# Attention followed by an expert layer: VectorE turns the summed head outputs in 32x32 blocks, reading the PSUM bank, where TensorE transposed ScalarE's copies of it

## What is computed

```python
y = einsum('bhqk,bhkd->bhqd', softmax(causal(q k^T / 4)), v)
y = y + einsum('bhqk,bhkd->bhqd', softmax(qc kc^T / 4), vc)
x = x + (y.reshape(B, T, C) @ Wp + bp)
x = x + expert_layer(layernorm(x))
```

## Time and profile before

| | |
|---|---|
| median of 3 runs | 1554.93 us |
| the profiled execution | 1567.87 us, its span 1565.1 us |
| PE busy | 1466.7 us (94%) |
| DVE busy | 1124.9 us (72%) |
| ACT busy | 907.4 us (58%) |
| POOL busy | 548.4 us (35%) |

### The profile page before, as it was taken

One profiled execution on the slowest core, in us unless ns is written; L12 is line 12 of the kernel. 1 busy time (PEld: TensorE's weight loads), 2 busy tenths in 40 slices (PEclk: granted clock), 3 DMA queues, 4 the chain that ended last, 5 costly groups with the idle time before them and its releaser, 6 DMA issues. The chain is left out here.

```text
span 1565.1 us, 26271 instructions
## 1 busy us (share of the span) xinstructions
PE 1466.7 (94%) x8868; PEld 717.5 (46%) x8868; DVE 1124.9 (72%) x3134; ACT 907.4 (58%) x1754; POOL 548.4 (35%) x1013
## 2 busy tenths in 40 slices
PE   8899999999999999999999999999998857999997
PEld 4443444444444444444453445344443323676674
DVE  7878887877888788778876887787785067455451
ACT  2177777677777777676777777767776500212211
POOL 4132333352344324332434333333213121443452
PEclk9599999999999999999999999999999877999999
DMA  6766483829374846575466738481900120444442
GB/s 189 121 142 84 89 111 103 118 66 147 101 106 85 144 103 103 98 157 82 91 116 125 100 81 127 106 117 63 138 4 3 42 86 14 117 99 123 119 99 50
DMA packets 82390, 155.25 MB, mean 99 GB/s; under 512 B 13008, under 2 KB 46416, under 8 KB 82256
## 3 DMA queue, kind: packets, MB, share of 16 engines
q1 hardware_dynamic: 74752, 142.43, 47.9%
q0 software_dynamic: 6144, 8.52, 3.2%
q10 hardware_dynamic: 1360, 2.62, 0.4%
HBM read 96.52 MB, written 53.08 MB: 96 GB/s over the span
## 5 line engine op out<-in xcount | busy, mean ns | idle before, releaser
L828 ACT ACTIVATE probs<-bank_ps 128x512 f32<-128x512 f32 (+1 forms) x1408 | 725.2, 579 | 236.7 <-PE bank_ps L610 229.9
L928 DVE TENSOR_REDUCE chunk_max<-bank_ps 128x1 f32<-128x512 f32 x1024 | 652.5, 684 | 125.2 <-PE bank_ps L649 122.4
L610 PE MATMUL bank_ps<-q_stack,k_stack 64*128 64x512 f32 (+3 forms) x1536 | 506.4, 422 | 41.2 <-ACT probs L828 37.3
L649 PE MATMUL bank_ps<-k_stack,q_stack 62*128 62x512 f32 (+3 forms) x1536 | 529.0, 432 | 7.0 <-DVE chunk_max L928 5.1
L649 PEld LDWEIGHTS bank_ps<-k_stack,q_stack 62*128 62x128 f32 x1536 | 248.8, 189 | 361.6 <-DVE chunk_max L928 211.5
L931 DVE CUSTOM_DVE_ANT_0 masked<-bank_ps,causal 128x128 bf16<-128x128 f32 (+3 forms) x512 | 233.4, 485 | 80.6 <-PE bank_ps L649 79.0
L610 PEld LDWEIGHTS bank_ps<-q_stack,k_stack 64*128 64x128 f32 x1536 | 235.1, 187 | 107.2 <-ACT probs L828 99.7
L1101 POOL TENSOR_TENSOR pool_idle<-pool_idle 128x1 f32<-128x1 f32 x292 | 57.0, 195 | 636.2 <-ACT probs L828 291.4
L628 PE MATMUL out_ps<-probs,v_cross 128*32 128x512 f32 x2048 | 277.1, 613 | 0.0
L1437 ACT ACTIVATE h<-h_ps,b1T 128x512 f32<-128x512 f32 x64 | 44.0, 687 | 227.3 <-PE h_ps L1369 227.3
L1369 PE MATMUL h_ps<-ff_yT,w1T 128*128 128x512 f32 x256 | 114.5, 601 | 0.6 <-DVE ff_yT L1450 0.6
(11 more groups left out here) (173 smaller groups left out, 1372.2 us busy)
## 6 DMA issues: line engine op xcount, KB each, us to landing
parts_dram<-parts SPq DMA_DIRECT2D x70, 512.0 KB, 2.7
k_stack<-parts_dram SPq DMA_DIRECT2D x180, 192.0 KB, 11.6
q_stack<-parts_dram SPq DMA_DIRECT2D x180, 128.0 KB, 10.6
w1T<-in_L_ffn_fc1s SPq DMA_DIRECT2D x8, 1024.0 KB, 5.7
w2T<-in_L_ffn_fc2s SPq DMA_DIRECT2D x8, 1024.0 KB, 7.4
z_rows<-z_sb SPq DMA_DIRECT2D x8, 528.0 KB, 13.9
x_sb<-in_x SPq DMA_DIRECT2D x8, 512.0 KB, 4.7
ctxT<-in_ctx SPq DMA_DIRECT2D x8, 512.0 KB, 11.6
```

The source lines that it names most:

```text
L610: mm = pe.matmul(bank_of(turn)[:, of.at:of.end], k_stack[base:base + SIDE, g, pair, of.keys:of.keys + P], q_stack[base:base + SIDE, g, pai ...
L649: return pe.matmul(bank[:, 0:n], q_stack[base:base + MAX_ROWS, g, pair, qc:qc + P], k_stack[base:base + MAX_ROWS, g, pair, k0:k0 + n], sta ...
L828: nc.scalar.activation(probs[:, buffer(u, i, p), side, columns], bank_of(("score", g, i, p, side))[:, columns], ACT.Exp, scale=SCALE)\
L928: nc.vector.tensor_reduce(dst, bank[:, 0:n], AX.X, ALU.max).then_inc(max_done, 1)
```

## The change

The turn of the sums moves from TensorE to VectorE. VectorE's transpose works in blocks of 32x32, in place among the partitions: each head's 32 partitions (16 channels, the denominator, 15 unused) become 32 columns, so the denominators lie along the free dimension as before. A query stands then on another partition than it would after a whole transpose; since a second turn puts it back, only the layouts of y_sb, y_add and rden change. To make the four heads' blocks of a unit fall at the right channels, a unit now holds heads h, h+2, ... of a half (head_in_half), and the loads from parts_dram pick those rows, in the same sizes.

- turn_heads: VectorE transposes out_ps (PSUM) into u_sb, behind maximum ahead_of_pieces of step 2 (causal part of the unit before) and of step 10 (context part). The value products of those steps now wait for turned, VectorE's semaphore. copy_out falls away.
- divide: VectorE's reciprocal and product, now from u_sb, at the places of OUTPUT_PLAN; GpSimd's addition follows at divide_self.
- turn_back: twice a batch VectorE turns y_sb into yT, and ScalarE adds the bias in place in SBUF (add_value_bias), where yT0 and yT1 were.
- The pieces out_cross, out_self, yT0, yT1 are gone, and PLAN is rearranged. Of the 44 steps of a batch, 28 had a piece besides "shift" before, and 19 have one now.
- Behind the loop VectorE also does the last addition; TensorE runs 8 matmuls of ones meanwhile (BEFORE_LAST).

```diff
-    (0, 2): (("vc0", 1),), (0, 3): (("out_cross", 0), ("out_self", 0)), (0, 4): (("v", 1),),
...
-    (3, 0): (("kc1", 1),), (3, 2): (("out_cross", 0),), (3, 3): (("k", 1), ("vc0", 0)), (3, 5): (("qc", 1),),
-    (3, 6): (("out_self", 0), ("zT1", 0)), (3, 7): (("shift", 0),), (3, 8): (("gate", 0), ("vc1", 0)),
+    (0, 2): (("v", 1),), (0, 3): (("vc0", 1),), (0, 5): (("y0T0", 0), ("y0T1", 0)), (0, 6): (("vc1", 1),),
+    (0, 7): (("shift", 0),), (0, 8): (("k", 0),), (0, 9): (("qc", 0),), (1, 1): (("kc1", 0),), (1, 2): (("q", 0),),
+    (1, 4): (("kc0", 0),), (1, 7): (("shift", 0),), (1, 10): (("proj0", 0),), (2, 1): (("proj1", 0),),
+    (2, 4): (("q", 1),), (2, 5): (("v", 0), ("vc0", 0)), (2, 7): (("shift", 0),), (2, 9): (("zT0", 0),),
+    (2, 10): (("kc1", 1), ("zT1", 0)), (3, 2): (("qc", 1),), (3, 3): (("k", 1),), (3, 4): (("kc0", 1), ("vc1", 0)),
+    (3, 6): (("gate", 0),), (3, 7): (("shift", 0),),
+}
+OUTPUT_PLAN = {
+    (0, 3): ("divide_cross",), (0, 5): ("divide_self",), (0, 8): ("turn_back",), (1, 2): ("divide_cross",),
+    (1, 4): ("divide_self",), (2, 3): ("divide_cross",), (2, 4): ("divide_self",), (2, 5): ("turn_back",),
+    (3, 2): ("divide_cross",), (3, 4): ("divide_self",),
 }
...
                 if i in (0, CROSS_IT) and (u > 0 or i > 0):
-                    pe.wait_ge(u_ready, 2 * u + (i > 0))
+                    pe.wait_ge(turned, 2 * u + (i > 0))
...
-            def copy_out(b, g, s):
-
-                u = UNITS * b + g
-                act.wait_ge(pv_done, ITS * u + (ITS if s else CROSS_IT))
...
-                nc.scalar.copy(u_sb[:, s, :], out_ps[:]).then_inc(u_ready, 1)
+            def add_value_bias(b, c):
+
+                act.wait_ge(turned_back, KT * b + c + 1)
+                nc.scalar.activation(yT[:, c, :], yT[:, c, :], ACT.Identity, bias=bias_v[:, 2, c:c + 1])\
+                    .then_inc(y_biased, 1)
...
+            def turn_heads(unit, s):
+
+                dve.wait_ge(pv_done, ITS * unit + (ITS if s else CROSS_IT))
+                nc.vector.transpose(u_sb[:, s], out_ps[:]).then_inc(turned, 1)
+
+            def divide(unit, s):
+
+                sums = u_sb[:, s].rearrange("p (n c) -> p n c", c=BLOCK)
+                dve.wait_ge(turned, 2 * unit + s + 1)
+                nc.vector.reciprocal(rden[:, s], sums[:, :, D]).then_inc(rden_done, 1)
+                if s:
+                    dve.wait_ge(y_done, unit)
+                dve.wait_ge(rden_done, 2 * unit + s + 1)
+                nc.vector.tensor_tensor(y_add[:] if s else heads_of(unit), sums[:, :, 0:D],
+                                        rden[:, s].unsqueeze(2).broadcast_to([P, T // BLOCK, D]),
+                                        ALU.mult).then_inc(y_part, 1)
+
+            def turn_back(b, c):
+
+                dve.wait_ge(y_done, UNITS * b + UNITS_HALF * (c + 1))
+                nc.vector.transpose(yT[:, c], y_sb[:, c].rearrange("p n c -> p (n c)")).then_inc(turned_back, 1)
...
                             if n == ahead_of_pieces(i):
+                                if i == BEHIND and UNITS * b + g > 0:
+                                    turn_heads(UNITS * b + g - 1, 1)
+                                elif i == CROSS_IT + BEHIND:
+                                    turn_heads(UNITS * b + g, 0)
+                                for name in outputs_at(first, g, i):
+                                    output(b, g, name)
                                 for at in pieces_at(first, last, g, i):
```

More of the change, by code:

```diff
@@ L57 @@
 V_PIECES = ("v", "vc0", "vc1")
-OUT_PIECES = ("out_cross", "out_self")
 PROJ_PIECES = ("proj0", "proj1")
-LATER = ("yT0", "yT1", *PROJ_PIECES, "zT0", "zT1", "gate")
+LATER = (*PROJ_PIECES, "zT0", "zT1", "gate")
 COL = {"q": (0, 512), "qc": (512, 1024), "k": (1024, 1536), "kc0": (1536, 2048), "kc1": (2048, 2560)}
@@ L85, in exists @@
         return not (last and g == UNITS - 1)
-    if name in OUT_PIECES:
-        return not (first and g == 0)
     if name in LATER:
@@ L105, with outputs_at @@
                          if name in HALF_PIECES and half == hf) for hf in range(2))
+def outputs_at(first, g, i):
+    return () if first and g == 0 else OUTPUT_PLAN.get((g, i), ())
 def pieces_at(first, last, g, i):
@@ L124, in piece_beside @@
     return n if a > 0 and a % PIECE_EVERY == 0 and n < len(PROLOGUE) - 1 else None
-EPILOGUE = (("out_cross", 0), ("out_self", 0), ("yT0", 0), ("yT1", 0), ("proj0", 0), ("proj1", 0), ("zT0", 0),
-            ("zT1", 0), ("gate", 0))
-MEANWHILE = {"out_self": 1, "yT1": 1, "proj1": 4, "zT1": 1}
+EPILOGUE = (("proj0", 0), ("proj1", 0), ("zT0", 0), ("zT1", 0), ("gate", 0))
+BEFORE_LAST = 8
+MEANWHILE = {"proj1": 4, "zT1": 1}
 def is_copied(name):
-    return not (name in COL or name == "shift" or name in OUT_PIECES or name in PROJ_PIECES)
+    return not (name in COL or name == "shift" or name in PROJ_PIECES)
 Piece = namedtuple("Piece", "name half of unit number copies")
@@ L392, in bank_of, with heads_of @@
             return bank_ps[:, SCORE_TURNS.index(turn) % SCORE_BANKS]
+        def heads_of(unit):
+            g = unit % UNITS
+            c = g % UNITS_HALF * D
+            return y_sb[:, g // UNITS_HALF, :, c:c + D]
         def buffer(u, i, pair):
@@ L676, in piece @@
                                       row_max[:, unit % 2].rearrange("p h s t -> p (h s t)"), ident[:])
-                elif name in ("out_cross", "out_self"):
-                    s = int(name == "out_self")
-                    pe.wait_ge(u_ready, 2 * unit + s + 1)
-                    mm = transpose4(bank, [u_sb[:, s, t * P:(t + 1) * P] for t in range(NT)])
-                elif name in ("yT0", "yT1"):
-                    pe.wait_ge(y_done, UNITS * b + UNITS)
-                    mm = transpose4(bank, [y_sb[:, t, c * P:(c + 1) * P] for t in range(NT)])
                 elif name in ("proj0", "proj1"):
+                    pe.wait_ge(y_biased, KT * b + KT)
                     for t in (0, 1):
@@ L751, in batch @@
                                 pe.wait_ge(*freed(find_piece(b, first, last, "y0T1")))
-                            elif at[2] == "proj0":
-                                pe.wait_ge(*freed(find_piece(b, first, last, "yT1")))
                             elif at[2] == "gate":
@@ L809, in _ @@
                     pe.wait_ge(*freed(epilogue_piece(B - 1, n - SCORE_BANKS)))
-                if name == "proj0":
-                    pe.wait_ge(*freed(epilogue_piece(B - 1, EPILOGUE.index(("yT1", 0)))))
-                elif name == "gate":
+                if name == "gate":
                     pe.wait_ge(*freed(epilogue_piece(B - 1, EPILOGUE.index(("zT1", 0)))))
@@ L881, in batch @@
                         exp_pair(b, g, i, 1)
-                        if i == BEHIND - 1 and g > 0:
-                            copy_out(b, g - 1, 1)
-                        elif i == BEHIND - 1 and not first:
-                            copy_out(b - 1, UNITS - 1, 1)
-                        elif i == CROSS_IT + BEHIND - 1:
-                            copy_out(b, g, 0)
+                        if "turn_back" in outputs_at(first, g, i):
+                            add_value_bias(b - (g == 0), int(g == 0))
             def store_parts(piece):
@@ L967, in added @@
             def added(piece, bank):
[L969 removed]
+                name, b = piece.name, piece.of
                 dve.wait_ge(piece_full, piece.number + 1)
[L971 to L988 removed]
@@ new lines, in added @@
+                c = PROJ_PIECES.index(name)
+                dve.wait_ge(xb_done, b + 1)
+                rows = x1[:, 2 * c:2 * c + 2, :].rearrange("p t c -> p (t c)")
+                nc.vector.tensor_tensor(rows, bank[:], rows, ALU.add).then_inc(proj_added, 1)
+            def turn_heads(unit, s):
[11 more added lines that the diff above has]
+                                        ALU.mult).then_inc(y_part, 1)
@@ L1080, in _ @@
             batch(B - 1, False, True, False)
+            turn_heads(UNITS * B - 1, 1)
+            for s in range(2):
+                divide(UNITS * B - 1, s)
+            dve.wait_ge(y_part, 2 * UNITS * B)
+            nc.vector.tensor_tensor(heads_of(UNITS * B - 1), heads_of(UNITS * B - 1), y_add[:], ALU.add).then_inc(y_done, 1)
+            turn_back(B - 1, 1)
             for n, (name, _) in enumerate(EPILOGUE):
```

75 lines of the change are left out of this document (27 added, 48 removed), and 4 rows, old and new, of the table PLAN.

## The result

The changed kernel takes **1604.08 us** in the median of four runs (1598.90 to 1607.13), the kernel before 1558.09 beside it: 1.0287 times as long (95% interval 1.0230 to 1.0344). The forecast was 1562, at most 1583. The profiled execution took 1601.61 us, its span 1599.9; before it was 1565.1.

The account below looks back on a forecast made before the run. TensorE was taken to bound steps with a piece, a chain of 2.70 us bare ones. Six middle batches +4.8, batch 0 +3.4, last batch -0.1, behind the loop -0.8: +7 us, 1562 us on the median; 8 in 10: 1541 to 1583.

Parts of the forecast that it names:

- The step that failed: SyncE's queue: as many transfers of the same sizes at the same places, listed among what costs nothing.
- The turn: VectorE's transpose of 128x512 floats from PSUM, taken as 0.69 us, plus 0.07 us for a hand-over.
- The wait in a bare step ten: TensorE waits 1.17 us for the turn behind the third maximum where no piece fills the time.
- The thin cover in (1, 10) and (2, 10): Pieces in these two steps make the products due 1.3 us later, covering the turn by 0.1 us.
- (2, 2): The only bare step 2 of a middle batch; TensorE waits 0.25 us there for the turn.
- Ten groups of transposes less, nine more bare steps: TensorE's part per batch: 6.3 us saved, 4.5 us lost to gaps of 0.5 us, so 1.8 us gained.
- Sum for a middle batch: -1.8 for TensorE, +2.34 for bare steps 10, +0.25 for a bare step 2: +0.8 us.
- Batch 0: First batch: 0.9 us saved on six groups, against waits in its steps 10 and (2, 2): +3.4 us.
- Behind the loop: From the last copy to the projection, 4.3 us instead of 5.09: -0.8 us.
- The free turn: Rival: waits for the turn vanish and only TensorE's saving stays, 1525 to 1540 us; 15%.
- The dearer turn: Rival: the turn takes 1.37 us, about +3.2 us a batch, +26 in all, 1588 us; 8%.
- The clock: Rival: clock falls in the waits of 16 bare steps 10, 1.54 us each, +25, 1587 us; 12%.

Follow-up runs that it names:

- e2: The changed kernel with SyncE's loads of slot 3 issued behind unit 1's shift instead of ahead of it and the context; 1571.36 us.
- e1: The changed kernel with the pieces gate and vc1 back at (3, 8) instead of (3, 6) and (3, 4); 1578.64 us.
- e4: The kernel before with only its plan changed: zT1 moved to (3, 2), vc1 to (3, 4), gate to (3, 6); 1576.99 us.
- e6: The kernel before with only the new order of heads (h, h+2, ... of a half) in fills, value products and y_sb; 1563.30 us.
- e7: e5 with the gate and vc1 back at (3, 8), as in e1; 1550.09 us.
- e5: e2 with VectorE's turn moved ahead of the first maximum of steps 2 and 10; 1555.66 us.
- e3: The kernel before with e2's reordering of SyncE's transfers; 1555.51 us.
- e9: e8 with five filler products of ones behind the last unit instead of eight; 1538.98 us.
- e8: e7 with a unit's heads on adjacent rows again, and Wp and the value biases laid out for the turned output; 1541.82 us.

## Why the prediction was wrong

**The step that failed** is the sentence that put SyncE's queue at nothing because it "has as many transfers of the same sizes at the same places". The places in SyncE's program were the same, but the time between them was not: I counted what the rearranged plan does to the length of a step, and not what it does to the length of the stretch between two shifts, into which a chain of transfers of nearly fixed length has to fit. The chain had next to no cover, and the queue showed it: in batches 2 to 6 of the kernel before unit 1's shift landed 7.6 to 11.8 us after its issue, where the shortest such time is 1.5, and three of these batches had waits of 1.15 to 1.22 us for it or for the context. The earlier trace rows even has one of them, which I read for its clock only, without asking what it waited for. The forecast had 0 us for it; it cost 33. Shown by e2 (only SyncE's order: -33 us, all waits for the shift gone), by e1 (only two pieces: -25) and by e4 (only three pieces, in the kernel before: +18); e6 shows that the new rows alone don't bring it. The Trainium skill (DMA: Bandwidth & Descriptors, "Queues, rings and completion order") says that the transfers that SyncE issues share one ring on each DMA engine and are taken from it in order; the trace agrees, with a 32 KB store that lands 14.0 us after its issue behind 1.9 MB of loads and 1.5 us after it without them.

**A second step failed the same way**: "the loads from parts_dram pick those rows, in the same sizes" is true, and I gave the rows no price anywhere. In the prologue they cost 9.1 us (e6: 8.8). The Trainium skill (SBUF — State Buffer, "Door 1: The DMA port swizzle") has a rule that would have spoken against it: partitions 32 apart lie on the same port. The two sides of a pair read rows 0 and 16 before and rows 0 and 32 now. By an estimate from the table of ports in that section of the Trainium skill, a group of six loads then reads from four ports instead of eight. SyncE took 4.39 instead of 3.75 us to issue such a group, and 11.21 instead of 7.82; that ports are the cause no run here shows apart.

**The parts that were summed**, by their terms:

- The turn: 0.69 forecast, 0.711 measured. The wait in a bare step ten: 1.17, measured 1.12 to 1.20 (3.95 against 2.75). The thin cover in (1, 10) and (2, 10) held in the middle batches: both are as long in e7 without the wait. (2, 2) was given 0.25 and takes 0.38 more than in e5. The waits for the turn stand in the steps that I named.
- Ten groups of transposes less, nine more bare steps: forecast -1.8 us a batch. An undisturbed batch takes 147.1 with the waits for the turn, 1.2 + 1.2 + 0.38 = 2.8, and 147.0 before, so this term was -2.7. In that it was too small; bare steps are 2.70 as before.
- Sum for a middle batch: +0.8 forecast, +0.1 measured (e2 against e3 as well: 147.0 to 147.1 against 146.8 to 147.1).
- Batch 0: +3.4 forecast, +0.8 measured. Its (1, 10) waits 0.70 and its (2, 10) not at all, where I had 1.17 and 0.55.
- Behind the loop: -0.8 forecast. I had the two turns' chain nearly right (from the turn at 1282.91 to the end of the bias at 1287.11 in the changed kernel, 4.2 us) and left out the eight products of ones, which TensorE ended at 1289.9. From turn to projection it took 6.83 us, where it was 5.09: +1.7. e9 shows it.

Without the two failed steps the number would have been near: e2 less the 8.3 us that e8 gave back stands at 1563. That is in part luck. Against e3, batches 1 to 6 of e2 are 6.1 us longer, where I had 4.8; but 5.0 of it is low clock behind the gate, which the forecast did not have, and the turn and the plan brought the other 1.1.

**The rivals.** The free turn didn't come about by itself, but e5 shows that a bound I had taken for fixed was not: I argued that "VectorE could not be earlier", since it needs the first tile 0.5 us after the step's start and three reductions follow. But VectorE need not have done the reductions first. Ahead of them it turns in time that it spends waiting otherwise: the turn of e5 starts 0.07 us behind the last value product (545.12 + 1.06 to 546.25). The dearer turn is out at 0.711 us. The clock: this rival came true in a few places. The clock fell to half at the end of a wait of 1.1 us for the turn or right behind it, with no wait for the shift near, twice in the changed kernel, four times in e1 and once in e2, of 15 such waits in each; a fall cost 1.1 to 1.2 us, in one case (e1, batch 6) 2.8. In the changed kernel that is 2.3 of the 46 us. The prediction named half clocks behind the waits as a sign of being wrong, and also said that a few may come; the 16 falls of the rival's price, +25, did not come. More of the low clock came where a wait for the shift, of 0.5 to 5.1 us, stood on top of the turn's, and behind the gate. The Trainium skill (TensorE: Matmul & The Clock Gate, "A second HAM failure mode") tells of a clock that goes to and fro over short idle times between groups of matmuls; the runs agree in part, with 7 falls behind 45 waits of 1.1 us.

**What stays open.** Whether e6 and the kernel before, with one plan and one queue, really differ in their waits for the shift. Why the clock falls behind the gate in some batches and not in others, and behind some of the turn's waits and not behind others. And what in the -2.7 us a batch is due to TensorE's transposes and what to the banks of the ring that they held.

## What to carry to other kernels

Moving pieces between steps changes the length of every stretch that they leave, also for engines that the change doesn't touch. For each queue with a chain that must be through by a certain step, read how long its last small transfer takes to land against the shortest such time in the trace. If it is several times that, it stands behind other transfers; then find the instruction that needs it and how much time is left (before, one such store landed after 7.6 us and nothing waited, another after 9.9 and TensorE waited 1.15 us). If little is left, the small urgent transfer belongs ahead of the large ones. And where a new layout alters which rows are read, price the transfers that read them, and try to put the permutation into weights instead.

## What the hardware did that I had not expected

- VectorE's transpose of 128x512 floats in 32x32 blocks takes 0.711 us from PSUM and 0.704 from SBUF, hardly more than a maximum over as many (0.68).
- SyncE took 3.75 or 4.39 us to issue six loads of the same sizes from SBUF to SBUF, and 7.82 or 11.21 in a busier moment, by which partitions they read (e6).
- The same wait of 1.1 us before the value products was followed by half clock in 7 cases of 45 (changed kernel, e1, e2), and a piece with the gate's eight columns alone in a step in two of six middle batches (changed kernel, e2) or in all six (e5).
